# Message-passing and mixture-of-experts kernel: a reordered routing tail and other node windows in the last step

## What is computed

```python
for _ in range(6):
    h = relu(f @ W1.T + b1) @ W2.T + b2
    msg = segment_sum(h[src], dst)
    r = sigmoid(xr + hr); z = sigmoid(xz + hz)      # xr.. from msg @ W_ih.T, hr.. from f @ W_hh.T
    f = (1 - z) * tanh(xn + r * hn) + z * f
x = x + f
x2 = layernorm(x)
vals, idx = top_k(x2 @ Wg + bg + bias, 2)
y = relu(x2 @ F1[e] + fb1[e]) @ F2[e] + fb2[e]      # for the two chosen experts e
x = x + sum of y weighted by softmax(vals)
```

## Time and profile before

| | us |
|---|---|
| median of three runs | 2192.18 |
| lowest and highest of them | 2184.37, 2199.14 |
| the profiled execution | 2198.43 |
| its span, first to last instruction | 2196.7 |
| PE busy in the span | 1910.3 |
| DVE busy | 1117.5 |
| ACT busy | 594.1 |
| POOL busy | 304.1 |

### The profile page before, as it was taken

How to read it: one execution, slowest core, us unless ns; L and a number is a source line. 1 busy time by engine, 2 the same in 40 slices (tenths; PEclk the granted TensorE clock), 3 DMA queues, 4 the chain that set the end, 5 groups by cost and what they waited for, 6 DMA issues and landing times.

```text
span 2196.7 us, 31507 instructions
## 1 busy us (share of the span) xinstructions
PE 1910.3 (87%) x11090; PEld 1129.8 (51%) x11091; DVE 1117.5 (51%) x2548; ACT 594.1 (27%) x1268; POOL 304.1 (14%) x434
## 2 busy tenths in 40 slices
PE   1666767999999999999999999999999998649991
PEld 1533334445654456445654457444664455439991
DVE  7589992344524445244533445244533655635555
ACT  0145552112221223112222123121221111126660
POOL 0012224554000000000000000000000112123331
PEclk7779998999999999999999999999999999769996
DMA  9900004342000000000000000000000000633225
GB/s 272 336 10 0 0 0 154 133 141 93 1 2 1 1 1 2 1 1 1 1 2 1 1 1 1 1 1 1 1 1 1 20 20 32 284 112 85 78 85 193
DMA packets 74392, 113.64 MB, mean 52 GB/s; under 512 B 10634, under 2 KB 63669, under 8 KB 73232
## 3 DMA queue, kind: packets, MB, share of 16 engines
q1 hardware_dynamic: 56618, 52.49, 8.0%
q0 software_dynamic: 12736, 39.29, 5.2%
q10 hardware_dynamic: 4902, 20.01, 2.3%
HBM read 49.99 MB, written 61.77 MB: 51 GB/s over the span
## 4 chain that ended last, share of the span: by engine, by line
PE 67%; DVE 15%; issue 9%; POOL 5%; ACT 1%; SPq 1%; DMA 1%; ACTq 1%; DVEq 0%; POOLq 0%
PE bank L1401 35%; PE bank L1425 24%; DVE hot_key L759 6%; PE bank L1385 4%; POOL chosen_out L563 3%; DVE hot_row L753 2%; POOL slot_in L542 2%; PE bank L1380 1%; PE bank L1299 1%; SPq L435 1%; PE bank L1469 0%; DMA y_pair<-chosen_out 0%; PE bank L1327 0%; PE bank L1462 0%; DVE r_lo L819 0%
## 5 line engine op out<-in xcount | busy, mean ns | idle before, releaser
L1401 PE MATMUL bank<-adj,r_hi 128*128 128x512 fp8e4 (+2 forms) x2100 | 732.6, 353 | 0.0
L1401 PE MATMUL bank<-adj,r_lo 128*128 128x512 fp8e4 (+2 forms) x2100 | 732.2, 353 | 0.0
L1401 PEld LDWEIGHTS bank<-adj,r_hi 128*128 128x128 f16 x2100 | 206.4, 98 | 190.5 <-issue 2.0
L1401 PEld LDWEIGHTS bank<-adj,r_lo 128*128 128x128 f16 x2100 | 206.4, 98 | 190.5 <-issue 1.7
L826 DVE SCALAR_TENSOR_TENSOR m_lo<-bank,msg_unit,m_hi 128x512 f16<-128x512 f32 (+2 forms) x84 | 57.3, 683 | 302.3 <-ACT m_hi L1112 302.3
L1327 PE MATMUL bank<-hot_key,hot_row 128*128 128x400 f16 x588 | 138.9, 351 | 60.5 <-DVE hot_key L759 58.1
L1425 PE MATMUL bank<-x_hi,wht_hi 128*128 128x512 f16 (+2 forms) x504 | 178.0, 353 | 9.2 <-DVE gate_a L844 9.2
L1425 PE MATMUL bank<-x_lo,wht_hi 128*128 128x512 f16 (+2 forms) x504 | 178.0, 353 | 0.0
L1425 PE MATMUL bank<-x_hi,wht_lo 128*128 128x512 f16 (+2 forms) x504 | 178.0, 353 | 0.0
L1425 PE MATMUL bank<-m_hi,wct_hi 128*128 128x512 f16 (+2 forms) x504 | 177.8, 353 | 0.0
L1425 PE MATMUL bank<-m_lo,wct_hi 128*128 128x512 f16 (+2 forms) x504 | 177.7, 353 | 0.0
(11 more groups left out here) (279 smaller groups left out, 2893.4 us busy)
## 6 DMA issues: line engine op xcount, KB each, us to landing
slot_in<-fill_rows SPq DMA_DIRECT2D x2, 13520.0 KB, 69.4
ffn_scratch<-pair POOLq DMA_DIRECT2D x32, 512.0 KB, 3.2
ffn_w<-ffn_scratch ACTq DMA_DIRECT2D x8, 2048.0 KB, 16.0
x_rows<-in_L_ffn_W POOLq DMA_DIRECT2D x32, 256.0 KB, 4.0
slot_x<-slot_in SPq DMA_DIRECT2D x30, 260.0 KB, 2.8
y_pair<-chosen_out SPq DMA_DIRECT2D x8, 640.0 KB, 9.0
xa<-in_x SPq DMA_DIRECT2D x1, 3072.0 KB
x<-in_x ACTq DMA_DIRECT2D x1, 3072.0 KB
```

Source lines behind the costliest of these rows:

```text
L1401: last = mm(bank[f][:, 0:n], r[:, q, f * P:(f + 1) * P], c, start=q == 0 and i == 0, stop=q == NT - 1 and i == len(todo) - 1)
```

## The change

**Windows.** The last step alone uses `END_TILES = (4, 4, 4, 4, 4, 3, 2)`; its last window has 182 columns in place of 310. The five steps ahead of it keep their windows (`cols`).

**POOL.** scale(w) stands ahead of scatter(w-1). The wait for `first_kept` is gone, since `choose` writes the first expert's id into `x2_rows` itself.

**DVE.** `choose` has 13 operations in a window for 18 (one more for the last window, where before it was two): two biases are added once ahead of the windows, and pairs of operations are fused. `place` has 5 operations whatever the number of tiles, for 2 a tile and 5. In exchange `prefix` on PE has 2 matmuls a tile for 2 in all; they add up the tiles before. gates(6, 0) stands ahead of normalise(5), and the last window's state goes to a buffer of its own, `x_end`. Three small operations are added at the start of the last step.

**Counts.** Every engine reads all eight counts once, ahead of its expert loop; SP does so before it waits for the scatters.

```diff
+END_TILES = (4, 4, 4, 4, 4, 3, 2)
...
+            def cols(s, w):
+                return (END_LEN[w], END_COL[w]) if s is LAST else (WIN_LEN[w], WIN_COL[w])
...
+            sp.wait_ge(sem("tiles_of"), 1)
+            counts = [sp.value_load(tiles_of[0:1, e:e + 1], min_val=1, max_val=CAP // TILE) for e in range(NX)]
...
             for i in range(2):
                 sp.wait_ge(sem(f"scattered{i}"), scattered_by(NW - 1 - (NW - 1 + i) % 2))
-            sp.wait_ge(sem("tiles_of"), 1)
...
             def scatter(w):
                 pool.wait_ge(sem("slot_of"), w + 1)
-                pool.wait_ge(sem("first_kept"), w + 1)
...
-            for w in range(NW - 2):
+            scale(0)
+            for w in range(1, NW):
                 scale(w)
-                scatter(w)
-            scale(NW - 2)
-            scale(NW - 1)
-            scatter(NW - 2)
+                scatter(w - 1)
             scatter(NW - 1)
...
-                a, z, xn = gate_a[:, 0:n], gate_z[:, 0:n], x_new[:, f, 0:n]
+                a, z, xn = gate_a[:, 0:n], gate_z[:, 0:n], (x_end if s is LAST and w == NW - 1 else x_new)[:, f, 0:n]
...
                     link(v.tensor_tensor(c, lg, over_experts(top[:, k, t0:t0 + nt], nt), ALU.is_equal))
-                    link(v.tensor_scalar(c, c, float(-NX), float(NX), ALU.mult, ALU.add))
-                    link(v.tensor_tensor(c, c, eid[:, 0:nt, :], ALU.add))
-                    link(v.tensor_reduce(first_id[:, k, 0:nt], c, AX.X, ALU.min))
-                    link(v.tensor_tensor(hot[k][:, 0:nt, :], eid[:, 0:nt, :], over_experts(first_id[:, k, 0:nt], nt), ALU.is_equal))
+                    link(v.scalar_tensor_tensor(c, c, float(-NX), eid_far[:, 0:nt, :], ALU.mult, ALU.add))
+                    link(v.tensor_reduce(first, c, AX.X, ALU.min))
+                    link(v.tensor_tensor(hot[:, k, 0:nt, :], eid[:, 0:nt, :], over_experts(first, nt), ALU.is_equal))
...
-            link(v.tensor_copy(filled[:], base[:]))
+            v.tensor_copy(filled[:], base[:]).then_inc(sem("filled"), 1)
+            v.tensor_scalar(eid_far[:], eid[:], float(NX), None, ALU.add)
...
+            gates(LAST, NW - 1, 0)
             normalise(NW - 2)
-            gates(LAST, NW - 1, 0)
             gates(LAST, NW - 1, 1)
...
+                for k in range(nt - 1):
+                    mm(earlier[:, k + 1:nt, :], all_ones[:], chosen[:, k:k + 1, :].broadcast_to([P, nt - 1 - k, NX]), start=False, stop=True, skip_group_check=True)
...
             logits(NW - 2)
+            rows(NW - 1)
             prefix(NW - 2)
-            rows(NW - 1)
```

125 lines of the change are left out of this document (68 added, 57 removed).

## The result

| | before | changed |
|---|---|---|
| median of 18 runs each, us | 2198.14 | 2179.01 |
| profiled execution, us | 2198.43 | 2180.43 |
| its span, us | 2196.7 | 2178.7 |
| first power of the last step, us | 1703.88 | 1702.57 |
| last scatter into `slot_in` starts, us | 1945.26 | 1923.81 |

The ratio of the two times is 0.9918, with an interval of 0.9906 to 0.993; one of the changed kernel's 18 executions was a slow one of 4721.8 us, and the ratio leaves it out. The forecast was 2164.9 us and faster by over 1%; measured are 19.1 us in the medians and 18.0 in the profiled executions, where 27.3 were forecast. The time lies inside the range (2151 to 2180), near its upper end. Of the 14.1 us between 2164.9 and 2179.0, 6.0 are none of the change's: the forecast started from 2192.18, the median of three runs, and the kernel before has 2198.14 over 18.

What follows compares the result with a forecast made beforehand. In the last step PE and DVE were held up by POOL's power queued behind scatters. Gain 14.6 us up to gates(5, 1), 26.7 by the last scatter, with counts 27.3: 2192.2 to 2164.9 us, range 2151 to 2180.

Steps and rivals of the forecast that it cites:

- power 5: Last step, POOL's power for normalise(5): forecast to end at 1887.1 us, before at 1903.3.
- the 16.0 and 7.2 us: Last step, windows 1 to 4: PE's waits before `columns` (16.0 us) and its low clock after them (7.2 us) go.
- the wait in front of rows(4): Last step, PE: a new wait of 2.3 us for DVE's last operations of gates(4, 1) and place(3).
- the largest term: Last step, windows 1 to 4: with the power ahead of the scatters, PE's waits (16.0 us) and low clock (7.2 us) go.
- The landing: Window 4's last scatter, under the weight loads: lands 8.5 us after issue, at 1904.6; normalise(6) on DVE waits for it.
- the 5 to 6 foretold: DVE at normalise(6): a wait of about 5 to 6 us for a DMA into `slot_in`, not for POOL.
- The first rival: Window 4's scatters land quickly, 2.4 us as in the quiet stretch: -33.0 us, 2159.2; chance 0.14.
- 3.8 and 1.0 us and the 2.7 of the new wait: Costs in the last step: window 4's wider gates 3.8, one tile more 1.0, PE's waits at rows(4) and `columns(4)` 2.7 us.
- The last stretch: Scatters of windows 5 and 6: POOL last by 1.0 us, last scatter starts at 1918.6 against 1945.26, gain 26.7 us.
- The counts: SP's count read and checks between last scatter's landing and expert loop: 0.6 us of path goes.
- 28 intervals of 6.49 us: Expert loop: taken as it is, 6.49 us a tile, no gain or loss.
- a worse rhythm: Rival, expert loop: half a us a tile more in POOL's round, 14.0 us, giving 2179; chance 0.09.

Runs made afterwards that it cites:

- before_new_pool_order: The kernel before with one edit: POOL takes the power of window w ahead of the scatters of window w-1; 2174.1 us, ratio 0.9897.
- third_row_buffer: The changed kernel with buffers of its own for window 6's rows and slots, so normalise(6) waits for no scatter; 2167.3 us, ratio 0.987.
- load_after_landing: The changed kernel, SP's tile load in the expert loop also waiting until the output rows of the tile four before have landed; 2178.3 us, ratio 0.993.
- last_two_loads_late: The changed kernel with the last two experts' weight loads issued behind ACT's copy of window 6's columns; 2172.9 us, ratio 0.989.
- seven_loads_late: The changed kernel with the weight loads of experts 1 to 7 issued behind ACT's copy of window 6's columns; 2184.8 us, ratio 0.996.
- end_tiles_4444333: The changed kernel with node tiles 4,4,4,4,3,3,3 in the last step too; 2175.3 us, ratio 0.991.

## Why the prediction was right and where it failed

**Up to power 5: right, in part by luck.** PE's waits in windows 1 to 4 went to nothing, as the 16.0 and 7.2 us had it, and the wait in front of rows(4) was 2.1 us for 2.3. Power 5 ended at 1887.24 for 1887.1; counted from the first power, which came 1.3 us earlier, it is 1.5 late. before_new_pool_order confirms the largest term by itself: from the first power to that of window 4 it takes 143.9 us for 165.9, so 22.0 for the 23.2.

There was a loss in it that I had not listed. PE's timeline of the changed kernel at gates(4):

```profile
1866.02 0.32 PE L1435 MATMUL bank<-x_hi,wht_lo 128*128 128x384 f16 x1 [0.81 <-issue]
...
1867.46 0.44 PE L1435 MATMUL bank<-m_lo,wct_hi 128*128 128x384 f16 x1 [0.47 <-issue]
1867.69 0.53 PE L1435 MATMUL bank<-m_hi,wct_lo 128*128 128x384 f16 x1
```

Two gaps of `issue` are followed by 3 us of matmuls at 0.53 for 0.33 us, at a granted clock of 0.50, the lower level. third_row_buffer and load_after_landing have the same work there without the gaps, and reach power 6 after 193.2 us for 197.0. What makes the gaps, no run tells. Without them power 5 ends 2.3 us ahead of the forecast, so the sum up to there was too cautious by about that, and two errors nearly cancelled.

**The landing: the step that failed.** "I take 8.5: landed at 1904.6." The last scatter of window 4 took 13.2 us and landed at 1909.77, so DVE waited 10.3 us for the 5 to 6 foretold, and the first tile load came at 1930.8 for 1926. The mechanism was in the forecast, with the place, the engine and the cause; the size was wrong. Of the 6.6 us missing at the last scatter (20.1 gained after the first power, for 26.7) the landing is 4.7 and the late issue 1.8, which is the gaps' 3.8 less the 2.0 by which the issue would have come early. last_two_loads_late and third_row_buffer show the landing as cause.

The forecast explained its 8.5 by scatters that met the end of six loads before and would meet their middle now. The trace of the kernel before says otherwise: its six loads, issued from 1881.2, had all landed only at 1916.3, and window 4's scatters landed between 1901.9 and 1911.7, so beside them from first to last. What went wrong is that DVE waits for the last scatter, and 8.5 is the median of six that land ever later. In the earlier trace rows the first of them is the 6.8; the last, asked for alone:

```profile
DMA to landing us min/median/max: 10.2/10.2/10.2
```

In load_after_landing, where the trace has each landing, window 4's eight go from 7.5 for the first to 12.4 for the last:

```profile
DMA to landing us min/median/max: 7.5/9.7/12.4
```

Why they fall behind shows in the changed kernel's DMA queues from 1892 to 1908 (packets, MB, share); q10 has the weight loads, q0 POOL's scatters:

```profile
q10 hardware_dynamic: 360, 5.14, 78.9%
q0 software_dynamic: 360, 1.03, 16.1%
q1 hardware_dynamic: 193, 0.18, 4.9%
```

The two queues moved the same number of packets, as they nearly did in the kernel before from 1899 to 1911 (292 and 287). A packet of the weights has 14.3 KB and one of the scatters 2.9 KB on average. So the scatters got 64 GB/s of 397, while POOL issues 133 KB every 1.27 us, which is 105 GB/s: as long as loads run, each scatter lands later behind its issue than the one ahead. From rows of the kernel before alone, 6.8 for the first and 0.68 more for each place make 11.6 for an eighth (an estimate), 3.1 of the 4.7 us. The other 1.6 stay open; q1 has no packets in the stretch of the kernel before. The packet counts come from the traces; no run changed the size of the packets.

The first rival, the rule of the Trainium skill ("DMA: Bandwidth & Descriptors", section "Anatomy of one DMA — SWDGE (gpsimd) path": 2.0 us and the bytes at 436 GB/s), was farther off under the loads: even with 4 MB less in flight the landing was 7.0 us behind the end of the issue. Where no load ran the trace agrees with it: in seven_loads_late the first six scatters of window 4 landed 2.4 to 2.7 us after their start, and the last two, beside 1 MB of `out_bias` loads, 5.3 and 4.6.

The new tiles were priced at 3.8 and 1.0 us and the 2.7 of the new wait. end_tiles_4444333 beside load_after_landing, both without the gaps, has window 4's first scatter only 4.0 us earlier after the first power, so these prices were too high. Two scatters fewer are issued in 2.4 us less, which the sum had. What it left out is that the last of six lands 10.6 us after its start, for 12.4 as the last of eight.

**The last stretch: right.** The scatters of windows 5 and 6 follow one another without a gap, POOL last and DVE in time. The counts: from the last scatter's start to the first tile load 7.46 and 7.43 us in the kernel before, 6.94 and 6.92 in the changed one, 7.45 and 7.47 with the reads back in the loop. So -0.5 for the forecast's -0.6.

**The expert loop: an average taken for a constant.** "28 intervals of 6.49 us" was one draw. The changed kernel's profile had 6.63 (+4.0 us), which is the rival "a worse rhythm" by a quarter; a second execution of the kernel before had 6.15. Against the profile, 6.6 of the 27.3 us forecast are missing in the tail and 4.0 in the loop, while an earlier first power gave 1.3: 18.0. Against the medians, in which the rhythm averages out, 8.2 are missing, 6.6 of them the tail. That split leans on one draw of the interval on each side. What exactly turns an execution into the slow rhythm stays open.

## What to carry to other kernels

When a wait goes, price the next one by the transfer that it really waits for: the last of its queue and not the median, under the traffic that it will meet then. Take a change apart before trusting its sum; here one reordering alone gave as much as all, and the parts together made DVE wait 10.3 us for a landing that with POOL's new order alone it did not wait for. Before two kernels are compared, look whether a stretch that neither edit touches runs alike in both: gaps at gates(4) made half of what the tiles seemed to cost. And profile the same program twice before reading a difference of some microseconds in a loop of two coupled transfers as an effect of an edit.

## What was not expected of the hardware

- Under the weight loads POOL's queue and the loads' queue moved the same number of packets (360 and 360 in 16 us), and with packets of 2.9 KB for 14.3 KB the scatters got 64 of 397 GB/s, less than POOL issued. So a scatter's landing depends on its place: from the start of the issue it took 2.4 us in a quiet stretch, and under the loads 6.8 us for the first and 10.2 for the last of six (before), 7.5 to 12.4 for eight (load_after_landing). With 14.7 MB issued behind the first scatters of window 5, the first tile load stood 26.4 us behind the last scatter's issue.
- Two transfers of a quarter of a MB, at a mean DMA share of 0.27, disturb each other: where the tile load came behind the end of the output's issue by half a us, 23 to 27 of 29 outputs landed in 1.5 us; where it came 0.3 to 1.9 us ahead, most took 1.6 to 3.8.
- The same program, profiled twice, differed by 9.4 us over 28 tiles, with late landings in one profile and few in the other.
- PE ran the same last step with gaps that the trace calls `issue` and without them, 3.8 us apart at power 6, when only the expert loop had been edited (changed kernel and load_after_landing). With other tile sizes in the last step the step's first power came at 1709.6 in two kernels, 5 to 7 us after the changed kernel's, and at 1706.9 in a third.
